# A ring of four chunks, VectorE four states at a time and later sums on TensorE in a state-space layer

## The reference

```python
u, z = split(x @ Win.T)                 # 512 inner channels each
uc = silu(conv4(u)); x_dbl = uc @ Wx.T  # 16 for the time step, 32 of B, 32 of C
dt = softplus(x_dbl[..., :16] @ Wdt.T + bdt)
def step(h, ins):                       # over 257 tokens; h is 512 channels x 32 states
    dt_t, B_t, C_t, u_t = ins
    dA = exp(dt_t[..., None] * A)
    h = dA * h + (dt_t * u_t)[..., None] * B_t[:, None, :]
    return h, einsum('bdn,bn->bd', h, C_t)
y = (ys + uc * Dp) * silu(z);  out = y @ Wout.T
```

## Time and profile before

| | |
|---|---|
| median of 3 runs | 3733.01 us (3732.58 to 3745.29) |
| the profiled execution | 3738.08 us, span 3736.3 us |
| share of the span busy | PE 85%, DVE 67%, ACT 55%, POOL 51% |
| the state-space layer | from about 1140 to 2995 us of the span |
| granted clock of PE | 0.941 over the span |

### The profile page before, as it was taken

The page is one execution under the profiler, slowest core; times in us unless marked ns, Lnnn a source line. Parts: engine busy times, 40 slices in busy tenths (PEclk is TensorE's granted clock), DMA queues, the critical chain, the costliest instruction groups (busy, mean ns, idle before and its releaser), DMA issues. The chain is left out here.

```text
span 3736.3 us, 61028 instructions
## 1 busy us (share of the span) xinstructions
PE 3177.2 (85%) x19916; PEld 2391.4 (64%) x19916; DVE 2509.6 (67%) x3780; ACT 2060.3 (55%) x4490; POOL 1907.3 (51%) x1672
## 2 busy tenths in 40 slices
PE   0959989989986889888888888898888887999957
PEld 0649976668974566666666666666665665666544
DVE  6351126653126999999999999999999833666541
ACT  0232225551226778777777778777777433666522
POOL 0013312200315898898888898988898600000024
PEclk9779989999997999999999999999999997999965
DMA  3039930012951111111111111111111000000036
GB/s 104 1 122 332 334 112 2 2 42 104 331 200 64 35 36 46 36 35 47 35 49 46 35 37 35 47 35 35 36 46 35 23 12 15 2 2 2 1 96 200
DMA packets 134796, 262.22 MB, mean 70 GB/s; under 512 B 13792, under 2 KB 106328, under 8 KB 123960
## 3 DMA queue, kind: packets, MB, share of 16 engines
q1 hardware_dynamic: 124568, 230.99, 18.8%
q0 software_dynamic: 9888, 27.01, 2.2%
HBM read 233.42 MB, written 24.55 MB: 69 GB/s over the span
## 5 line engine op out<-in xcount | busy, mean ns | idle before, releaser
L2013 POOL TENSOR_TENSOR ssm_hc<-ssm_hs,ssm_cb 128x1024 f32<-128x1024 f32 x512 | 1205.3, 2358 | 178.0 <-PE ssm_py L2127 157.9
L2513 DVE TENSOR_TENSOR_SCAN ssm_hs<-ssm_da,ssm_pb 128x512 f32<-128x512 f32 x1024 | 1222.0, 1208 | 96.0 <-POOL ssm_hc L2013 91.3
L2127 PE MATMUL ssm_py<-ssm_hc,ident 128*128 128x256 f32 x4096 | 1069.2, 384 | 39.2 <-POOL ssm_hc L2013 39.2
L2326 ACT ACTIVATE ssm_da<-ssm_dt,ssm_an 128x255 f32<-128x255 f32 x2048 | 863.8, 498 | 194.1 <-DVE ssm_hs L2513 155.5
L2127 PEld LDWEIGHTS ssm_py<-ssm_hc,ident 128*128 128x128 f32 x4096 | 709.8, 192 | 119.4 <-POOL ssm_hc L2013 47.2
L2494 DVE TENSOR_TENSOR ssm_pb<-ssm_pb,ssm_dtu 128x512 f32<-128x512 f32 x832 | 563.7, 678 | 49.1 <-PE ssm_pb L2114 25.6
L2114 PE MATMUL ssm_pb<-ssm_bst,ssm_eyeb 96*128 96x256 bf16 x1664 | 327.9, 279 | 140.3 <-DVE ssm_hs L2513 121.8
L2114 PEld LDWEIGHTS ssm_pb<-ssm_bst,ssm_eyeb 96*128 96x128 bf16 x1664 | 133.1, 99 | 346.2 <-DVE ssm_hs L2513 248.7
L3353 DVE TENSOR_TENSOR moe_hid<-moe_pu,moe_actg 128x512 f32<-128x512 f32 x71 | 49.1, 692 | 349.1 <-PE moe_pu L2988 349.1
L2988 PEld LDWEIGHTS moe_pu<-moe_xt,moe_up 128*128 128x128 f32 x2272 | 266.8, 193 | 6.4 <-ACT moe_xt L3113 3.0
L2988 PE MATMUL moe_pu<-moe_xt,moe_up 128*128 128x128 f32 x2272 | 267.8, 277 | 1.8 <-ACT moe_xt L3113 1.8
(11 more groups left out here) (591 smaller groups left out, 5195.8 us busy)
## 6 DMA issues: line engine op xcount, KB each, us to landing
moe_up<-in_moe_up SPq DMA_DIRECT2D x72, 1024.0 KB, 6.1
ssm_cb<-ssm_c_dram SPq DMA_DIRECT2D x64, 1024.0 KB, 5.6
moe_down<-in_moe_down SPq DMA_DIRECT2D x72, 512.0 KB, 7.1
sw_wt<-in_sw_w SPq DMA_DIRECT2D x64, 192.5 KB
moe_x_dram<-moe_tok SPq DMA_DIRECT2D x32, 128.0 KB
moe_yg<-moe_y_dram SPq DMA_DIRECT2D x16, 256.0 KB, 3.3
tok_w<-in_wd SPq DMA_DIRECT2D x4, 576.0 KB, 12.8
out<-h SPq DMA_DIRECT2D x1, 2056.0 KB, 6.4
```

Of the source, the lines that this page charges most:

```text
L2013: nc.gpsimd.tensor_tensor(hc[:, n % 2, part_], hs[:, n % 2, part_], cb[:, q % 2, part_, :], ALU.mult).then_inc(s["hc_done"], 1)
L2127: ins = nc.tensor.matmul(sums(j), k.ident[:], hc[:, n % 2, st, :], start=False, stop=(q == QN - 1 and st == NQ_ - 1 and j % 2 == 1))
L2326: ins = nc.scalar.activation(da[:, n % 2, 2 * m + o, 1:L], dt2[:, v, j, 1:L], ACT.Exp, scale=a_n[:, d, j, st:st + 1])
L2513: nc.vector.tensor_tensor_scan(two(hs[:, n % 2, 2 * m:2 * m + 2, :]), two(da[:, n % 2, 2 * m:2 * m + 2, :]), two(pb[:, p % 4]), 0.0, ALU.m ...
```

## The change

`hs` now holds four chunks (RING = 4) and `hc` is gone: POOL multiplies by C in place in `hs`. It does so when both halves of the chunk have been scanned, and after a wait for its own copy of the last states. PE's `total` runs three chunks behind (BEHIND = 3) and reads `hs`; a scan of chunk `n` waits for the `total` of chunk `n - 4`. DVE's product and scan take four states, 1024 columns in two banks, so that `pb` has two places; the product comes directly ahead of its own scan. PE signals the spread after the second pair of states, and ahead of the first waits for the scan before the last one. Turned are now four states, the second half of the chunks in quarters 1 and 3. `products` on ACT makes 16 instructions for a unit where it made 12. `out_chunk` goes from chunks 0 and 2 to 1 and 3, `last_gate` from chunk 2 to 3.

```diff
+    RING, BEHIND = 4, 3
...
-        hs = sb("hs", [P, 2, NQ_, L])
-        hc = sb("hc", [P, 2, NQ_, L])
+        hs = sb("hs", [P, RING, NQ_, L])
...
-        TURNED = (1, 2, 3)
+        PAIRS = SUB // 2
+        TURNED = (1, 3)
...
-        def turned(p):
-            return p % 4 == TM and p // 4 // DJ in TURNED
+        def turned(r):
+            return r % 2 == 1 and r // 2 // DJ in TURNED
...
+                        pool.wait_ge(s["scanned"], scanned(2 * n + 2))
+                        if n == 3 and before is not None:
+                            last_gate(u - 1, 1 - v)
+                        settle(pool, k)
+                        nc.gpsimd.tensor_copy(h_l[:, v, j, q * NQ_:(q + 1) * NQ_], hs[:, n % RING, :, L - 1]).then_inc(s["h_kept"], 1)
+                        pool.wait_ge(s["h_kept"], Turn(u, NCH)(n + 1))
                         for half in range(2):
...
-                            pool.wait_ge(s["b_free"], scanned(4 * n + 2 * half + 2))
-                            if half == 0:
-                                pool.wait_ge(s["y_free"], summed(n - 1))
...
-                            nc.gpsimd.tensor_tensor(hc[:, n % 2, part_], hs[:, n % 2, part_], cb[:, q % 2, part_, :], ALU.mult).then_inc(s["hc_done"], 1)
+                            part_ = hs[:, n % RING, 4 * half:4 * half + 4, :]
+                            nc.gpsimd.tensor_tensor(part_, part_, cb[:, q % 2, 4 * half:4 * half + 4, :], ALU.mult).then_inc(s["hc_done"], 1)
...
                 def spread_b(u, v, p):
 
-                    if turned(p):
+                    r = p // 2
+                    if p % 2 == 0 and (r >= 2 or not (isinstance(u, int) and u == 0)):
+                        pe.wait_ge(s["scanned"], Turn(u, PAIRS)(r - 1))
+                    if turned(r):
                         turn_products(u, v, p)
                         return
                     if p == 0:
                         pe.wait_ge(s["stacked"], u + 1)
-                    pe.wait_ge(s["b_free"], Turn(u, SUB, 4)(p - 3))
...
-                    ins.then_inc(s["b_done"], 1)
+                    if p % 2:
+                        ins.then_inc(s["b_done"], 1)
...
-                            if n >= 2:
-                                total(u, v, d, n - 2, m)
+                            if n >= BEHIND:
+                                total(u, v, d, n - BEHIND, m)
...
-                            free = Turn(u, SUB, 4)(4 * (n - 1) + m + 1) if n or before is not None else None
+                            free = Turn(u, PAIRS)(2 * (n - 1) + m // 2 + 1) if n or before is not None else None
...
+                def product(u, v, r):
+
+                    j, at = r // 2 % DJ, 2 * (r % 2)
...
+                    dve.wait_ge(s["b_done"], Turn(u, PAIRS)(r + 1))
+                    b4 = pb[:, at:at + 2].rearrange("p g s t -> p (g s) t")
+                    nc.vector.tensor_tensor(b4, b4, dtu2[:, v, j:j + 1, 0:L].broadcast_to([P, 4, L]), ALU.mult).then_inc(s["b_set"], 1)
+
+                def scan(u, r):
+
+                    n, half = r // 2, r % 2
+                    if half == 0 and (n >= RING or not (isinstance(u, int) and u == 0)):
+                        dve.wait_ge(s["y_free"], Turn(u, NCH, 2)(n - RING + 1))
+                    dve.wait_ge(s["da_done"], Turn(u, SUB)(2 * r + 2))
...
+                    nc.vector.tensor_tensor_scan(four(hs[:, n % RING]), four(da[:, n % 2]), steps, 0.0, ALU.mult, ALU.add).then_inc(s["scanned"], 1)
...
+                    for r in range(PAIRS):
+                        n = r // 2
+                        if not turned(r):
+                            product(u, v, r)
+                        scan(u, r)
```

More of the change, by code:

```diff
@@ L1830, in section_mamba, with made @@
         SUB = 4 * NCH
-        TM = 3
-        TURNED = (1, 2, 3)
+        PAIRS = SUB // 2
+        TURNED = (1, 3)
         def sums(j):
             return py[:, j // 2, j % 2 * L:j % 2 * L + L]
-        def turned(p):
-            return p % 4 == TM and p // 4 // DJ in TURNED
-        def made(p):
-            return sum(not turned(i) for i in range(p + 1))
+        def turned(r):
+            return r % 2 == 1 and r // 2 // DJ in TURNED
+        def made(r):
+            return sum(not turned(i) for i in range(r + 1))
         def image(u, d):
@@ L2227, in _ @@
                 last = UN - 1
-                for n in (NCH - 2, NCH - 1):
+                for n in range(NCH - BEHIND, NCH):
                     for m in range(4):
@@ L2337, in take_steps, with products @@
                         nc.scalar.copy(dtut[:, h, :], pm[:, h, :]).then_inc(s["dtut_in"], 1)
-                def products(u, v, q, o, free):
-                    if o == 0:
+                def products(u, v, q, i, free):
+                    if i == 0:
                         act.wait_ge(s["last_out"], u + 1)
@@ L2345, in products @@
                             act.wait_ge(s["b_done"], free)
[L2346 to L2350, removed]
+                    for o in range(2):
+                        st = q * NQ_ + 4 + 2 * i + o
+                        for h in range(2):
+                            ins = nc.scalar.activation(tp[:, i, o, h, :], dtut[:, h, :], ACT.Copy, scale=bt[:, v, h, st:st + 1])
+                    ins.then_inc(s["tp_in"], 1)
                 def decay_last(u):
@@ L2377, in body @@
                             take_steps(u)
[L2378 to L2384, removed]
+                        if n in (1, 2):
+                            products(u, v, 1, n - 1, Turn(u, PAIRS)(0) if before is not None else None)
+                        if n in (8, 10):
+                            products(u, v, 3, n // 2 - 4, Turn(u, PAIRS)(PAIRS // 2))
                         if after is not None:
@@ new lines, in product @@
+                    b4 = pb[:, at:at + 2].rearrange("p g s t -> p (g s) t")
[5 more added lines that the diff above has]
+                    dve.wait_ge(s["da_done"], Turn(u, SUB)(2 * r + 2))
+                    if turned(r):
+                        dve.wait_ge(s["b_done"], Turn(u, PAIRS)(r + 1))
+                    else:
+                        dve.wait_ge(s["b_set"], Turn(u, made(PAIRS - 1))(made(r)))
+                    steps = pb[:, 2 * half:2 * half + 2].rearrange("p g s t -> p (g s t)")
+                    four = lambda ap: ap[:, 4 * half:4 * half + 4, :].rearrange("p s t -> p (s t)")
+                    nc.vector.tensor_tensor_scan(four(hs[:, n % RING]), four(da[:, n % 2]), steps, 0.0, ALU.mult, ALU.add).then_inc(s["scanned"], 1)
@@ L2514, in body @@
+                def body(u, v, d, before, after):
+                    for r in range(PAIRS):
[3 more added lines that the diff above has]
+                        scan(u, r)
+                        for m in (2 * (r % 2), 2 * (r % 2) + 1):
                             if before is not None:
-                                if n in (0, 2) and m in (1, 2):
-                                    out_chunk(u - 1, 1 - v, before, n + m - 1)
+                                if n in (1, 3) and m in (1, 2):
+                                    out_chunk(u - 1, 1 - v, before, n + m - 2)
```

54 lines of the change are left out of this document (12 added, 42 removed).

## The result

The changed kernel takes 3753.43 us (median of 20 runs, 3733.64 to 3770.52), the kernel before 3734.96 us on the same chips (20 runs, 3716.45 to 3751.53). The ratio is 1.005, with a 95% interval of 1.0031 to 1.0069: 18 us slower. Forecast were 3694 us, faster. The time lies in the range that was given, but the kernel became slower where it was to become faster.

The account below looks back on a forecast made before the run. DVE was taken to bound the kernel, POOL and PE close behind. 102.9 + 6.6 + 1.0 = 110.5 us a unit against 113.1, times 16, less 3 at the ends, saves 39 us: 3694 us, range 3640 to 3765.

Parts of the forecast that it names:

- DVE's work: DVE's own products and scans, counted from start to start: 102.9 us a unit after the change, against 104.6.
- The self-wait: On DVE, a scan directly behind its own product waits for its end: 24 x 0.13 = 3.1 us a unit.
- the merge: DVE's products and scans of four states instead of two: only 1.7 us a unit gained, eight multiplied states fewer included.
- two sentences: Skill's rules for DVE: about 150 cycles fixed per instruction (9.4 us a unit saved); semaphores between instructions free (some 45 us).
- POOL's chunk and the ring: POOL takes 4.9 us a chunk in place; the ring's slack removes DVE's 6.3 us of waits for POOL.
- PE's stalls in quarter 1, ACT and fuse: DVE's stalls a unit: 4.75 us for PE, 1.85 for ACT's four decays, 1.0 for `fuse` ahead of product r = 26.
- The place that comes due next is `dt_set` for `turn_steps` at (0,1): POOL's lag at a unit's start: `dt_set` comes 27.8 us after chunk 11, 1.8 us remain, no stall.
- signs of being wrong: Waits for `ssm_py` or `dt_set` at unit starts, clock under 0.98, POOL's product over 2.36, PE waits in quarters 0 and 2.
- The ends: First scan needs four decays, 0.8 us; POOL takes its last chunk whole, 5.1 instead of 2.8: together 3 us lost.
- (A): Rival: PE's lateness is absorbed, DVE and POOL run at their floors, 104.4 us a unit, 3597 us; chance 0.12.
- (B): Rival: slower, DVE waits for PE's jobs between spread halves, 13.8 us a unit, up to 3794 us; chance 0.22.
- (C): Rival: waits only move, stalls of 9 to 11 us a unit return the gain in quarter 1, 3715 to 3750; chance 0.2.

Follow-up runs that it names:

- a_outlast: The changed kernel with only `out_last` moved from (2,0) to (3,0): 3714.35 us, ratio 0.9949 to the kernel before.
- b_ring: The kernel before with the four-chunk ring alone (POOL in place, `total` three chunks behind), two states, `out_last` at (2,0): 3719.44 us, ratio 0.9972.
- b_ring_outlast: The kernel before with the four-chunk ring alone, two states, and `out_last` moved to (3,0): 3668.74 us, ratio 0.9824 to the kernel before.
- b_four: The changed kernel's four states and turned halves on the old two-chunk `hs` and `hc`, no ring: 3795.58 us, ratio 1.0169 to the kernel before.
- a_ahead: The changed kernel with `out_last` at (3,0) and each next half's product issued ahead of this half's scan: 4789.05 us in one run.

## Why the prediction was wrong

**DVE's work: right.** The forecast was 1.25 us from a product to its scan, 2.19 for a scan, 3.44 for a half. The rows above give 1.25, 2.20 (1478.52 to 1480.72) and 3.45. The self-wait is 1.25 - 1.14 = 0.11 us, where 0.13 were assumed. The forecast saving was 1.7 us a unit; the table has 2.9 less busy time, of which 24 x 0.04 = 1.0 come back as gaps between product and scan. What the forecast calls the merge is more than paid for by the four products fewer, 4 x 0.58 = 2.3 us: by the same starts the width alone makes DVE's work 0.6 us longer (24 x 1.25 + 32 x 2.19 against 48 x 0.58 + 64 x 1.12). In the changed kernel a fifth of the products stand 1.31 to 1.37 us ahead of their scan and not 1.25 (last section); that is 0.4 us a unit that the forecast did not have.

The Trainium skill ("VectorE: DVE Perf Modes") offered two sentences against this count, and neither came true here. By the section on the TRN2 errata each instruction that is dropped saves a fixed latency; two scans of 512 columns take 2.24 us from start to start and one of 1024 takes 2.20. By the section on the DRAIN a semaphore costs nothing extra; the wait for the instruction directly ahead costs 0.11 us. (The forecast's own figure for that wait, 24 x 0.13 us in 16 units, is 50 us and not 45; the sum does not use it.)

**POOL's chunk and the ring: right as far as they went.** The scan's waits for POOL, 6.3 us a unit, are gone. A chunk takes POOL 4.9 us (1419.43 to 1424.32 in the unit shown), as forecast. `dt_set` comes 28.0 us after the end of chunk 11 in that unit (1386.56 to 1414.60), forecast 27.8; PE waits 0.6 us for it, and no wait of DVE comes of that.

**PE's stalls in quarter 1, ACT and fuse: right.** The hand-made order gave stalls of 1.75, 0.4, 1.7, 0.1 and 0.8 us and 1.85 for ACT. One unit of the changed kernel:

```profile
1457.59 1.23 DVE L2491 TENSOR_TENSOR ssm_pb<-ssm_pb,ssm_dtu 128x1024 f32<-128x1024 f32 x1 [1.62 <-PE ssm_pb L2114]
...
1461.49 2.29 DVE L2505 TENSOR_TENSOR_SCAN ssm_hs<-ssm_da,ssm_pb 128x1024 f32<-128x1024 f32 x1 [0.35 <-PE ssm_pb L2098]
...
1465.40 1.23 DVE L2491 TENSOR_TENSOR ssm_pb<-ssm_pb,ssm_dtu 128x1024 f32<-128x1024 f32 x1 [1.62 <-PE ssm_pb L2114]
...
1471.91 1.23 DVE L2491 TENSOR_TENSOR ssm_pb<-ssm_pb,ssm_dtu 128x1024 f32<-128x1024 f32 x1 [0.75 <-PE ssm_pb L2114]
```

and 1.93 for ACT in the row at 1475.07. (A wait in brackets counts from the end of the record ahead, some 0.1 us later than the count by starts.) `fuse` shows as one wait of 0.93 us, forecast 1.0:

```profile
2081.45 1.23 DVE L2491 TENSOR_TENSOR ssm_pb<-ssm_pb,ssm_dtu 128x1024 f32<-128x1024 f32 x1 [0.93 <-PE ssm_pb L2114]
```

Without the missed wait these terms hold: a_outlast takes 111.04 us a unit, forecast 110.5. Of the 0.54 between them 0.4 are the longer distances ahead of the scans.

**The step that failed: "The place that comes due next is `dt_set` for `turn_steps` at (0,1)."** The ring lets POOL fall behind, and I followed what hangs on a late POOL to one consumer only; the sum, 102.9 + 6.6 + 1.0, has waits for POOL at nothing. But `dt_set` is not the place that comes due next, `out_last` is. The same count, carried on by chunks 14, 15 and 0 and `last_token` (2.3 us, 1429.23 to 1431.51), would have led to `out_last` at (2,0): there DVE needs a result of `last_token` that this POOL has only 2 us later. Before, the first scan of chunk 2 waited until POOL had done chunk 0, behind which `last_token` stands directly, and in the trace of that kernel DVE came for the result well after it was there:

```profile
1406.10 0.46 POOL L1986 TENSOR_TENSOR ssm_tl<-ssm_tl,ssm_bcl 128x128 f32<-128x128 f32 x1
...
1410.08 0.26 DVE L2471 TENSOR_REDUCE ssm_yl<-ssm_tl 128x4 f32<-128x128 f32 x1
```

With PE's idle time and the lower clock behind it this is 2.95 us a unit (a_outlast), 3.05 with two states (b_ring against b_ring_outlast). It makes 2.95 of the 3.5 us by which the unit was missed. Of the signs of being wrong that I had named, one showed: a wait for PE in quarter 0, the 1.65 us at 1440.69. The wait at the start of units came too, but for neither `ssm_py` nor `dt_set`. The clock in the layer was 0.98 and not under it; this mean hides a few microseconds at half the clock in most units.

**The ends: 3 forecast, 7.8 measured.** From POOL's first start in the layer to PE's first matmul behind it the kernel before takes 2995.2 - 1134.4 = 1860.8 us, the changed one 3032.1 - 1150.7 = 1881.4. Of these 20.6 us the fifteen periods give 12.8. The stretch ahead of the first row gives 5.1 (118.9 against 113.8) and the one behind the last 2.7 (52.6 against 49.9). The one behind, where POOL takes its last chunk whole, is near the forecast of 2.3. Ahead of the first row 0.8 were forecast. There 18 products stand 0.08 us further ahead of their scans than 1.25, 1.4 us, and POOL's first record in the layer (L1935) lasts 3.40 us and not 2.23. The rest of the 5.1, and the reason for that record, stay open.

**The rivals.** (A) did not happen. (B) was said to decide from 10.2 us of stalls a unit. There are (86.0 + 27.9 + 25.6 + 3.9) / 14.04 = 10.2 of them in the window 1300 to 2900 (with the row at its end):

```profile
DVE ssm_pb L2491 <- PE ssm_pb L2114: 86.0, 70, 2.5
DVE ssm_hs L2505 <- ACT ssm_da L2327: 27.9, 17, 1.9
DVE ssm_yl L2468 <- POOL ssm_tl L1986: 25.6, 13, 3.7
DVE ssm_hs L2505 <- PE ssm_pb L2098: 3.9, 11, 0.4
```

The outcome is thus at the border of (B) and (C), but by neither's mechanism; 8.4 of the 10.2 are for PE and ACT, and without the other 1.8 neither case would have been reached. Of (B)'s 13.8 us of jobs that DVE would wait for, those of quarters 0 and 2 stayed hidden but for the one at (2,0) to (3,0).

**Ring or width.** The four kernels with and without each, all with `out_last` at (2,0), have 113.14 (neither), 112.41 (ring), 116.89 (width) and 113.99 us (both). With `out_last` at (3,0) the ring alone has 109.36 and both have 111.04. So the ring, with all that belongs to it, is the half that pays: 3.8 us a unit at two states once `out_last` is moved. The width costs 1.6 to 3.75 us whatever stands beside it. In the table it takes 1.3 to 3.1 us off DVE's busy time and adds 3.3 to 6.5 to its idle time: PE and ACT have to deliver four states at once where two would do to go on.

## What to carry to other kernels

A deeper ring between two engines removes a wait by permitting a lag: list every consumer of the lagging engine's other results, not only those of the ring, and place each as late as the lag. Merging instructions is counted from start to start, and it coarsens every handover around it; where DVE already waited for its suppliers, the coarser step cost more than the saved starts. A short idle stretch of PE is not priced by its length alone; look at the durations of the matmuls behind it.

## What the runs showed of the hardware

After an idle time of PE its next matmuls ran at the granted clock's lower level in some cases and not in others, and the length of the idle time alone does not tell which. At `out_last` in the changed kernel idle times of 2.7 to 5.4 us were followed by groups of four matmuls of up to 1.91 us in 12 units, and by groups of 1.03 us in two (3.40 and 3.07 us idle). In the kernel before PE waits 2.3 us for `tp` once a unit; between 1300 and 2900 us groups of 1.91 us follow 3 of these 14 waits, and groups of 1.03 us the others.

The distance from a product to the scan that needs it is not the same everywhere. In the changed kernel it is 1.24 to 1.27 us for most, but 1.31 to 1.37 in the first unit, from 1984 to 2208 us and in the last unit, with the same records:

```profile
2049.08 1.21 DVE L2491 TENSOR_TENSOR ssm_pb<-ssm_pb,ssm_dtu 128x1024 f32<-128x1024 f32 x1
2050.39 2.29 DVE L2505 TENSOR_TENSOR_SCAN ssm_hs<-ssm_da,ssm_pb 128x1024 f32<-128x1024 f32 x1
```

In such a unit 24 products cost some 2 us more. a_outlast and b_four show it in nearly the same stretches (1927 to 2147 and 1984 to 2199 us in the middle). In a_ahead, where no scan needs the instruction directly ahead, the distance is 1.13 to 1.15 us in the whole layer. What causes it stays open.
